# Summing the gate parts of a four-chain LSTM recurrence with two additions in place of one reduction, and longer loop bodies on three engines

## What is computed

```
def step(carry, xt):
    h, c = carry
    zg = xt @ Wi + h @ Wh + b
    i, f, g, o = jnp.split(zg, 4, axis=-1)
    c = jax.nn.sigmoid(f) * c + jax.nn.sigmoid(i) * jnp.tanh(g)
    h = jax.nn.sigmoid(o) * jnp.tanh(c)
    return ((h, c), h)
```

## Time and profile before

| what | value |
|---|---|
| median of 3 runs | 6249.12 us (6246.4 to 6255.38) |
| the profiled execution's own time | 6250.81 us |
| its span, first to last instruction | 6248.8 us |
| granted TensorE clock, mean over the span | 0.964 |
| PE busy | 5595.9 us (90%) |
| DVE busy | 4774.4 us (76%) |
| ACT busy | 2351.6 us (38%) |
| POOL busy | 1726.4 us (28%) |
| HBM traffic | 302.7 MB, 48 GB/s over the span |

### The profile page before, as it was taken

How to read it: one execution, slowest core, us unless ns; L and a number is a source line. 1 busy time by engine, 2 the same in 40 slices (tenths; PEclk the granted TensorE clock), 3 DMA queues, 4 the chain that set the end, 5 groups by cost and what they waited for, 6 DMA issues and landing times. The chain is left out here.

```text
span 6248.8 us, 161662 instructions
## 1 busy us (share of the span) xinstructions
PE 5595.9 (90%) x59552; PEld 2263.0 (36%) x59552; DVE 4774.4 (76%) x14157; ACT 2351.6 (38%) x8487; POOL 1726.4 (28%) x8205
## 2 busy tenths in 40 slices
PE   7978788889899897999999999999999999998895
PEld 4545423233333232333333333333333333333443
DVE  4545676667576766999999999999999999994224
ACT  2334354355454444333333333333333333333332
POOL 0000000000000000555555555555555555552000
PEclk9989989999999998999999999999999999999997
DMA  0003443343432444011101110111101111012110
GB/s 12 0 24 129 127 80 78 95 73 74 94 74 64 93 89 139 19 34 20 34 14 34 20 34 24 24 34 20 34 14 34 33 21 34 14 20 69 35 68 10
DMA packets 378689, 303.02 MB, mean 48 GB/s; under 512 B 146073, under 2 KB 358681, under 8 KB 373562
## 3 DMA queue, kind: packets, MB, share of 16 engines
q1 hardware_dynamic: 378510, 301.15, 20.3%
HBM read 182.09 MB, written 120.59 MB: 48 GB/s over the span
## 5 line engine op out<-in xcount | busy, mean ns | idle before, releaser
L1300 PE MATMUL bank<-lparts,lstate 128*32 128x512 bf16 x49152 | 3006.1, 383 | 214.8 <-POOL lstate L1387 96.5
L1300 PEld LDWEIGHTS bank<-lparts,lstate 128*32 128x32 bf16 x49152 | 1133.0, 97 | 2088.2 <-POOL lstate L1387 1183.1
L1312 DVE STREAM_TRANSPOSE ltz<-bank 128x512 f32<-128x512 f32 x2048 | 1464.9, 715 | 129.8 <-PE bank L1300 51.4
L1357 ACT ACTIVATE lgate<-lz 128x48 f32<-128x48 f32 x2048 | 497.9, 243 | 2078.5 <-DVE lz L1318 2077.1
L1318 DVE TENSOR_REDUCE lz<-ltz 128x64 f32<-128x256 f32 x2048 | 1270.6, 620 | 0.0
L1051 DVE TENSOR_REDUCE bnegmax<-bank 128x1 f32<-128x512 f32 x1024 | 649.8, 680 | 251.2 <-PE bank L981 250.3
L1384 POOL TENSOR_TENSOR lstate<-lstate 128x16 f32<-128x16 f32 x2048 | 439.4, 215 | 1324.4 <-DVE lstate L1332 1250.4
L1270 POOL MEMSET lstate<- 128x256 f32 x1 | 0.3, 312 | 2471.4 <-POOLq L61 2471.4
L1096 ACT ACTIVATE wh<-bank 128x512 f32<-128x512 f32 x1024 | 554.4, 598 | 295.3 <-PE bank L1003 288.3
L1394 POOL COPY ltz<-wh 128x64 f32<-128x64 f32 x2048 | 593.6, 290 | 0.0
L883 PE MATMUL bank<-xT,bw 128*128 128x512 f32 x1024 | 537.0, 626 | 56.7 <-DVE bzs L894 51.7
(11 more groups left out here) (209 smaller groups left out, 4365.9 us busy)
## 6 DMA issues: line engine op xcount, KB each, us to landing
zx<-bzs SPq DMA_DIRECT2D x32, 2048.0 KB, 6.8
wh<-zx SPq DMA_DIRECT2D x64, 1024.0 KB, 8.7
bqp<-qk SPq DMA_DIRECT2D x198, 128.0 KB, 4.7
bkp<-qk SPq DMA_DIRECT2D x198, 128.0 KB, 7.9
qk<-eparts SPq DMA_DIRECT2D x96, 256.0 KB, 2.6
hs<-wh SPq DMA_DIRECT2D x32, 512.0 KB, 6.0
cmemT<-hs SPq DMA_DIRECT2D x32, 512.0 KB, 4.4
bw<-in_w_attend SPq DMA_DIRECT2D x4, 2304.0 KB, 11.4
```

What stands on the lines that cost most here:

```text
L1300: last = nc.tensor.matmul(bank[x][32 * q:32 * q + 32, :], top[:, x, k].rearrange("p m r -> p (m r)"), parts[:, way, g, k, n, q], start=k = ...
L1312: nc.vector.transpose(out, bank[x][:].rearrange("p (e n c) -> p e n c", e=2, n=8)).then_inc(turned[x], 1)
L1357: nc.scalar.activation(gate[:, x], z[:, x, :, 0:3], ACT.Sigmoid)
```

## The change

The reduction of L1318 becomes two `tensor_tensor` additions on DVE. `sum_pairs` adds rows m = 1, 2 to rows m = 3, 4, 128 results a partition, in which 4 neighbouring elements (the sequences) are innermost; it takes over both waits. `sum_halves` adds the two halves, 64 results, and signals `summed`; it waits for `paired`, a new semaphore. `cell` of chain x-1 stands between them. A tile `lhalf` of 512 words a partition holds what lies between. The loop bodies grow: PE and DVE to 8 steps (64 turns), ACT to 16 steps (32 turns). GpSimd and SP stay as they are.

```diff
-UNROLL = 4
+PE_STEPS, DVE_STEPS, ACT_STEPS = 8, 8, 16
...
+        half = core.sb(ctx, "lhalf", [P, chains, 2, 2 * BLOCKS, B])
...
-                with pe.Fori(0, S // UNROLL) as turn:
-                    for i in range(UNROLL):
+                with pe.Fori(0, S // PE_STEPS) as turn:
+                    for i in range(PE_STEPS):
                         for x, (way, g) in enumerate(CHAINS):
-                            pe.wait_ge(ready[x], UNROLL * turn + i + 1)
+                            pe.wait_ge(ready[x], PE_STEPS * turn + i + 1)
...
-                def sum_parts(x, t):
+                def sum_pairs(x, t):
                     dve.wait_ge(placed[x], t + 1)
                     dve.wait_ge(turned[x], t + 1)
-                    rows = tz[:, x].rearrange("p (j m r) -> p j m r", j=16, r=ROWS_OF_8)[:, :, 1:5, 0:4]
-                    nc.vector.tensor_reduce(z[:, x].rearrange("p e g (s b) -> p (e g s) b", b=B),
-                                            rows.rearrange("p j m b -> p j b m"), AX.X, ALU.add).then_inc(summed[x], 1)
+                    rows = tz[:, x].rearrange("p (j m r) -> p m j r", j=2 * BLOCKS, r=ROWS_OF_8)[:, 1:5, :, 0:B]
+                    nc.vector.tensor_tensor(half[:, x], rows[:, 0:2], rows[:, 2:4], ALU.add).then_inc(paired[x], 1)
+
+                def sum_halves(x, t):
+                    dve.wait_ge(paired[x], t + 1)
+                    nc.vector.tensor_tensor(z[:, x].rearrange("p e g (s b) -> p (e g s) b", b=B), half[:, x, 0],
+                                            half[:, x, 1], ALU.add).then_inc(summed[x], 1)
...
-                with dve.Fori(0, S // UNROLL) as turn:
-                    first = UNROLL * turn
-                    for i in range(UNROLL):
+                with dve.Fori(0, S // DVE_STEPS) as turn:
+                    first = DVE_STEPS * turn
+                    for i in range(DVE_STEPS):
                         for x in range(chains):
...
                             turn_products(x, first + i)
                             multiply(x1, t1)
                             new_state(x2, t2)
-                            sum_parts(x, first + i)
+                            sum_pairs(x, first + i)
                             cell(x1, t1)
+                            sum_halves(x, first + i)
...
-                with act.Fori(0, S // UNROLL) as turn:
-                    first = UNROLL * turn
-                    for i in range(UNROLL):
+                with act.Fori(0, S // ACT_STEPS) as turn:
+                    first = ACT_STEPS * turn
+                    for i in range(ACT_STEPS):
```

More of the change, by code:

```diff
@@ L1217, in four @@
             return core.sems("ls", " ".join(f"{name}{x}" for x in range(chains)))
-        (made, turned, summed, gated, multiplied, celled, tanhed, stated, rest1, ready, placed) = (
-            four(n) for n in ("made", "turned", "summed", "gated", "multiplied", "celled", "tanhed", "stated", "rest1",
+        (made, turned, paired, summed, gated, multiplied, celled, tanhed, stated, rest1, ready, placed) = (
+            four(n) for n in ("made", "turned", "paired", "summed", "gated", "multiplied", "celled", "tanhed", "stated", "rest1",
                               "ready", "placed"))
```

## The result

The changed kernel takes 6262.9 us (median of 12 runs, 6256.28 to 6272.63) against 6250.64 for the kernel before (12 executions too, one of which took 11856.63 us and is left out of the ratio); the ratio is 1.0021, with a 95% interval of 1.0012 to 1.0030. It is slower by 0.2%, some 13 us, and the interval excludes a ratio of 1. The forecast was no change, at 6247; the time lies in the stated range (6225 to 6320), on the side of rival 1.

A forecast was written before the change was run, and what follows sets the result against it. A 3.05 us ring for 2 slots through DVE, GpSimd and PE was taken as the bound. 6250.8 us + 0 (additions) - 2 (bodies) = 6249, 6247 against the median: no change likeliest (0.64), range 6225 to 6320.

The forecast's parts named there:

- rival 1: GpSimd's two subtractions slowed by DVE's two-input additions: slower, 6298 us in one form, 6431 in another; chance 0.19.
- The ring: Transpose, `new_state`, GpSimd's two subtractions, PE's matmuls, next transpose: 3.05 us for 2 slots, claimed to set the pace.
- 132 + 250: DVE's idle time in the recurrence stretch, 132 us before, forecast to rise by some 250 us.
- rival 2: Longer loop bodies on PE or DVE stall on instruction fetch: 64 ends cost 435 us, 6682 us; chance 0.05.
- the one that put the additions at 0: The two DVE additions replacing the reduction free about 0.12 us a slot, worth 0 on the path.
- small form of rival 1: Subtractions held only while an addition reads: 0.05 us a ring, 51 us, 6298; three quarters of the 0.19 chance.
- the large: Each GpSimd subtraction waits until the addition is over: 0.18 us a ring, 184 us, 6431 us.
- the near miss: `sum_pairs` reads until 0.95 us after the transpose, just short of the first GpSimd subtraction's start at 0.96.
- Rival 3: Reduction on the path after all, DVE's floor holding slots: faster, 6073 us, or 6230 in a small form; chance 0.12.
- the large forms: Outcomes outside the range: 6431 us (subtractions wait), 6682 (fetch stalls), 6073 (reduction on the path); together about 0.2.

The follow-up runs named there:

- e3_pairs_256: Changed kernel with `sum_pairs` covering all 8 words of each row, 256 results in place of 128: 6390.03 us, ratio 1.0228 to the kernel before.
- e7_state_first_on_after: Changed kernel with `new_state` moved ahead of `multiply` on DVE: 6252.39 us, ratio 1.0004 to the kernel before.
- e8_state_first_on_before: Kernel before, reduction kept, with `new_state` moved ahead of `multiply` on DVE: 6164.19 us, ratio 0.9866 to the kernel before.
- e5_cell_last: Changed kernel with `cell` moved after `sum_halves`: 6261.65 us, ratio 1.0024 to the kernel before.
- e4_pairs_64: Changed kernel with `sum_pairs` adding only row 1 to row 3, 64 results: 6286.35 us, ratio 1.0065 to the kernel before.
- e6_pairs_64_cell_last: Changed kernel with 64 results in `sum_pairs` (row 1 plus row 3) and `cell` after `sum_halves`: 6250.24 us, ratio 1.0003 to the kernel before.

## Why the prediction was wrong

**What held.** The ring bounds both kernels: the pace follows it to 0.01 us in e3_pairs_256 and e7_state_first_on_after, and shortening it helps where nothing holds GpSimd (e8_state_first_on_before), until DVE is full. The reduction is off the path: with it gone DVE's idle time went from 132 us to 388 (3196 less 2808), where 132 + 250 was forecast. The additions took 293 and 226 ns against 290 and 220. `sum_halves` started at 1.15 and not 1.21 us after the transpose, for the wait for `paired` costs less than the 0.10 that I took from the transpose. ACT's table loads fell from 128 to 32 at no gain, and GpSimd's loop ends kept their stalls (33.2 us, had 37.0). No stall of fetching appeared on PE or DVE (rival 2).

**The step that failed** is the one that put the additions at 0, with rival 1 at 0.19: "L1387 overlaps `cell` in almost every slot today, and takes 215 ns as L1384 does". Those rows were right, and told less than I took from them. `cell` starts 0.10 us after the second subtraction, and the runs show that an addition which starts 0.03 us or more after a subtraction doesn't hold it (16 elements in `cell`, 64 in `sum_halves`); what holds is one that started first. The trace before had no subtraction with an addition started just ahead of it, so it bounded nothing, and the ring had no slack: the margin was 12 ns a ring. The hold measured 17 ns a ring, where the small form of rival 1 had 50 and the large 180. By the sentence found in the runs it would have been sized at once: `sum_pairs` ends at 1.11 us, so the first subtraction at 1.19 and not at 1.17. `sum_halves`, which I had charged with the rest, started before the second subtraction too (1.15 against 1.26) but ends at 1.38; 1.38 + 0.08 is 1.46, and the second subtraction ends at 1.47 unheld.

The mechanism of rival 1's small form fits the runs, but it was charged in the wrong place. It said that a subtraction is held while the addition reads, until 0.82 + 128 x 1.05 ns = 0.95 us, "just short of 0.96", and laid its 0.05 us mainly on `sum_halves`. If a held subtraction is taken to need its unheld 215 ns once it is let go, the medians of the traces say when that is: 0.15 us after the start of `sum_pairs` with 128 results (changed kernel, e5_cell_last, e7_state_first_on_after), 0.28 with 256 (e3_pairs_256), and 0.03 after the start of `cell` with 16 (e4_pairs_64, and the second subtraction in e6_pairs_64_cell_last). That makes an estimate of 1.04 ns an element, beside the 1.05 of the earlier trace rows, and some 17 ns on top; it is the sentence on the ends, told from the start of the addition. So `sum_pairs` let go at 0.97 us and not at 0.95: the near miss was a hit, by 16 ns, and `sum_halves`, which started 0.06 us sooner than I had it, missed.

The Trainium skill ("SBUF — State Buffer", Who interferes with whom) has the rule that an instruction of VectorE with two SBUF inputs contends with a GpSimd instruction that reads SBUF, and `tensor_reduce` does not. The runs agree: 215 ns beside the reduction, 231, 331 and 362 beside `sum_pairs` as it overlaps more. In the prediction I let one row with a late start count against it.

**Rival 3** gets nothing: PE's gap ahead of every second burst of matmuls stayed (0.13 us on the median, before and after). That the hold goes through a shared read port is the account of the Trainium skill ("SBUF — State Buffer", Who interferes with whom); what the runs show is the timing of the hold. No run here put an addition with one of its inputs outside SBUF in that place.

One sum was off: the large forms that the stated range left out had less together than "about 0.2". Rival 1's had 0.05, rival 2 had 0.05, and rival 3's was the less likely part of 0.12.

## What to carry to other kernels

Find the ring first, and then ask of each new instruction not only how long it takes on its own engine but what it overlaps on the engines that are in the ring; freed time on a busy engine outside of it is worth nothing, as long as it stays outside (in e8_state_first_on_before the ring got so short that DVE was full). When a row is used against a contention, look at which of the two started first, and which ended last. An exchange of two independent lines inside the ring gave 1.3% where replacing the costliest instruction of the stage gave a loss.

## What the runs showed that I had not expected

- GpSimd's subtraction, when held, ended 0.07 to 0.08 us after `sum_pairs` in the changed kernel, e3_pairs_256, e5_cell_last and e7_state_first_on_after, whether it had itself started 0.03 or 0.14 us behind it, and 0.08 after `cell` in e4_pairs_64 and e6_pairs_64_cell_last: the hold has an end that doesn't move with the start.
- DVE seems to be held too, though no run was made for it. `cell` takes 165 ns in the kernel before and 168 to 169 where it starts with a subtraction or just ahead of one (e4_pairs_64, e6_pairs_64_cell_last). Where it starts 0.03 to 0.21 us behind a subtraction that is still running, its end falls 0.03 us after the end of that subtraction: 184 ns in the changed kernel, e3_pairs_256 and e7_state_first_on_after, 215 in e5_cell_last. In e8_state_first_on_before, where it takes 209, it starts 0.03 behind `keep_state`. In the kernel before it starts 0.11 behind the second subtraction, ends 0.06 after it and isn't longer.
- `new_state` takes 165 ns with `multiply` before it and 131 ns straight behind the transpose; `multiply` takes 150 ns straight behind the transpose and 181 behind `new_state` in e7_state_first_on_after. So it is the second place that costs some 32 ns, whichever of the two has it. Why was not tried.
- No run has a `sum_halves` that ends late enough to hold the second subtraction; that it would follows from the same sentence, which `cell` bears out in e6_pairs_64_cell_last.
